# The routers of three expert layers, each as one stage, and one normalisation on GpSimd beside its router

## The reference, cut to what matters

```python
# layer 0: a layer normalisation of the input without gain, and in the layer a second one
mu = mean(x); var = mean((x - mu) ** 2); u = (x - mu) / sqrt(var + 1e-5)
logits = u @ router_W + router_b                    # 1024 x 8
gates = softmax of the two largest logits, at their experts
xhat = (u - mean(u)) / sqrt(var(u) + 1e-5)          # the experts' input
# layer 1
probs = softmax(u @ router_w.T)                     # over all 8
gates = the two largest probs, at their experts
# layer 2
gate = u @ W_gate
mask = softmax(where(gate >= second largest, gate, -inf))
out = mean over the experts of (relu(u @ W1 + b1) @ W2 + b2) * mask
```

## Time and profile before

| | |
|---|---|
| median of 3 runs | 4622.57 us (4617.99 to 4632.91) |
| profiled execution, its own time | 4627.87 us |
| its span, first to last instruction | 4626.1 us |
| mean granted TensorE clock | 0.961 of full speed |
| PE busy | 4177.0 us (90%) |
| PEld busy | 3167.9 us (68%) |
| DVE busy | 2563.9 us (55%) |
| ACT busy | 1782.1 us (39%) |
| POOL busy | 848.0 us (18%) |

### The profile page before, as it was taken

The page is one execution under the profiler, slowest core; times in us unless marked ns, Lnnn a source line. Parts: engine busy times, 40 slices in busy tenths (PEclk is TensorE's granted clock), DMA queues, the critical chain, the costliest instruction groups (busy, mean ns, idle before and its releaser), DMA issues. The chain is left out here.

```text
span 4626.1 us, 107755 instructions
## 1 busy us (share of the span) xinstructions
PE 4177.0 (90%) x44428; PEld 3167.9 (68%) x44428; DVE 2563.9 (55%) x5138; ACT 1782.1 (39%) x3751; POOL 848.0 (18%) x556
## 2 busy tenths in 40 slices
PE   8989999999888989999976789886899999999987
PEld 5669998999667956666642379752699766666465
DVE  4468777777253055555539832246443466665454
ACT  2245555555222424444534312120254344444221
POOL 1222222221101200000029611006222100000201
PEclk9999999999988999999988899898899999999999
DMA  1010000000104821111012168649111000000100
GB/s 35 27 36 18 17 17 17 17 17 1 49 1 174 306 74 44 45 45 45 17 47 78 46 253 314 247 158 141 51 45 54 22 31 24 24 24 10 39 15 10
DMA packets 137827, 305.05 MB, mean 66 GB/s; under 512 B 51800, under 2 KB 87584, under 8 KB 119744
## 3 DMA queue, kind: packets, MB, share of 16 engines
q1 hardware_dynamic: 132992, 287.01, 19.7%
q0 software_dynamic: 4416, 12.06, 0.8%
HBM read 273.46 MB, written 23.47 MB: 64 GB/s over the span
## 5 line engine op out<-in xcount | busy, mean ns | idle before, releaser
L3070 DVE TENSOR_REDUCE block_max<-PS 128x1 f32<-128x512 f32 (+1 forms) x896 | 505.3, 626 | 300.7 <-PE PS L2930 299.9
L3019 ACT ACTIVATE probs_turned<-PS 128x512 f32<-128x512 f32 (+1 forms) x896 | 434.7, 570 | 562.8 <-PE PS L2951 562.7
L1149 PE MATMUL PS<-context_turned,queries 128*128 128x422 f32 (+2 forms) x1536 | 335.3, 360 | 4.8 <-ACT probs L1218 1.9
L1181 PE MATMUL PS<-probs_turned,context_part 128*128 128x256 f32 (+1 forms) x2496 | 327.7, 285 | 2.2 <-DVE weighted L1260 2.2
L1210 ACT CAST probs_turned<-PS 128x512 fp32r<-128x512 f32 (+1 forms) x512 | 232.4, 511 | 229.2 <-PE PS L1161 229.2
L1226 DVE TENSOR_TENSOR probs_turned<-PS,probs_turned 128x512 fp32r<-128x512 f32 (+1 forms) x512 | 276.5, 581 | 75.0 <-ACT probs_turned L1210 73.1
L1181 PEld LDWEIGHTS PS<-probs_turned,context_part 128*128 128x128 f32 (+1 forms) x2496 | 304.2, 189 | 2.4 <-DVE probs_turned L1226 2.4
L2971 PEld LDWEIGHTS PS<-probs_turned,values 128*17 128x17 f32 x13312 | 191.6, 97 | 150.1 <-issue 123.5
L1149 PEld LDWEIGHTS PS<-context_turned,queries 128*128 128x128 f32 x1536 | 262.5, 191 | 32.9 <-ACT probs L1218 9.0
L1218 ACT ACTIVATE probs<-PS,minus_max 128x844 f32<-128x844 f32 (+1 forms) x256 | 238.6, 932 | 105.1 <-DVE minus_max L1271 103.9
L2930 PE MATMUL PS<-keys_turned,queries 32*128 32x512 f32 (+1 forms) x2048 | 241.4, 548 | 40.9 <-ACT probs_turned L3019 35.9
(11 more groups left out here) (542 smaller groups left out, 7507.4 us busy)
## 6 DMA issues: line engine op xcount, KB each, us to landing
context_rows<-in_ctx SPq DMA_DIRECT2D x40, 768.0 KB
context_turned<-ctx_turned SPq DMA_DIRECT2D x32, 800.5 KB
routed_up<-in_L_ffn_W SPq DMA_DIRECT2D x23, 1024.0 KB, 7.9
routed_down<-in_L_ffn_W SPq DMA_DIRECT2D x23, 1024.0 KB, 6.0
routed_up<-in_L_ffn_wg_w SPq DMA_DIRECT2D x23, 1024.0 KB, 7.7
routed_second<-in_L_ffn_w_w SPq DMA_DIRECT2D x23, 1024.0 KB, 10.2
routed_down<-in_L_ffn_w_w SPq DMA_DIRECT2D x23, 1024.0 KB, 5.1
v_all<-v_turned SPq DMA_DIRECT2D x128, 128.0 KB, 17.5
```

What stands on the lines that cost most here:

```text
L1149: last = nc.tensor.matmul(PS[:, j, 0:cols], qs[a][:, v, p * P:(p + 1) * P], yT[b][:, v, at:at + cols], start=(m == 0), stop=(m == 2))
L1181: last = nc.tensor.matmul(O_ps, yp[a][0:kk, u, k, :], probsT[b][0:kk, par, k, :], start=(k == 0 and m == 0), stop=(k == KT - 1 and m == 2))
L3019: nc.scalar.activation(probs[0:kk, t % ring, i, 0:many].rearrange("p k c s -> p (k c s)"), PS[0:kk, bank_of("turned", t, i), 0:many * 2 * ...
L3070: nc.vector.tensor_reduce(part[:, b % 2, chunks[0]:chunks[-1] + 1, i, u // 2], bank, AX_X, ALU.max).then_inc(max_done.sem, 1)
```

## The change

Each router becomes one stage. `Router` issues the sixteen matmuls into one PSUM bank (bank 0, eight columns a tile), signals once, and lets two spare products follow; ScalarE begins the stage with a one-element exponential and later takes the exponential of the scores; VectorE does all the rest, reading the scores from PSUM. `two_of_scores` (layer 0), `two_of_softmax` (layer 1) and `kept_gates` (layer 2) hold VectorE's list. In layer 0 `linear_normal` now keeps moments and both inverse deviations, U takes the plain one, and the stage `normalize(core, U, hat)` is gone: GpSimd makes `hat` from the residual by a subtraction and a multiplication in the router's stage. `uT` of layers 0 and 1 stays allocated for the whole layer. Here is the diff, cut to its core (the lines of `top_two` that went are those described above).

```diff
@@ -447,7 +447,7 @@
                     for t in tiles:
                         if gain is None:
-                            nc.vector.tensor_scalar(dst[:, t, :], X[:, t, :], moments[:, t, 0:1], rstd[:, t:t + 1],
+                            nc.vector.tensor_scalar(dst[:, t, :], X[:, t, :], moments[:, t, 0:1], (both[:, 1] if with_plain else rstd)[:, t:t + 1],
                                                     ALU.subtract, ALU.mult).then_inc(step.sem, 1)
@@ -1727,39 +1727,195 @@
-def top_two(core, own, scores, iota):
...
+class Router:
+    def __init__(self, core, own, w, bias=None):
...
+        self.scores = core.sb(own, "scores", [P, TILES, EXPERTS])
+        self.ready, self.step = core.semaphore("rows_ready"), core.semaphore("vector_step")
+        self.shifted, self.exps = core.semaphore("scores_shifted"), core.semaphore("exps_ready")
+        self.products = core.PS[:, 0, 0:TILES * EXPERTS].rearrange("p (t e) -> p t e", e=EXPERTS)
+    def tensor_program(self, core, pe, src):
+        wait_weights(core, pe)
+        for t in range(TILES):
+            for c in range(DC):
+                last = core.nc.tensor.matmul(core.PS[:, 0, t * EXPERTS:(t + 1) * EXPERTS], src[:, c, t * P:(t + 1) * P], self.w[:, c, :],
+                                             start=(c == 0), stop=(c == DC - 1))
+        last.then_inc(self.ready.sem, 1)
+        spare_products(core, BANKS - 1, 2)
+    def scalar_program(self, core, act, x):
+        core.nc.scalar.activation(self.warm[:], core.ident[0:1, 0:1], ACT.Exp)
+        act.wait_ge(self.shifted.sem, self.shifted.at(1))
+        core.nc.scalar.activation(x, x, ACT.Exp).then_inc(self.exps.sem, 1)
+    def wide(self):
+        return self.top[:].unsqueeze(2).broadcast_to([P, TILES, EXPERTS])
...
+class TopTwo:
...
+    def find(self, core, dve, step, past, scores):
+        nc = core.nc
+        for t in range(TILES):
+            nc.vector.max(self.best[:, t, :], scores[:, t, :]).then_inc(step.sem, 1)
+        dve.wait_ge(step.sem, step.at(past + TILES))
+        for t in range(TILES):
+            nc.vector.max_index(self.place[:, t, :], self.best[:, t, :], scores[:, t, :]).then_inc(step.sem, 1)
+        dve.wait_ge(step.sem, step.at(past + 2 * TILES))
+        nc.vector.tensor_copy(self.placef[:], self.place[:]).then_inc(step.sem, 1)
+    def mark(self, core, dve, step, past):
+        dve.wait_ge(step.sem, step.at(past))
+        for n, out in enumerate((self.first, self.second)):
+            core.nc.vector.tensor_tensor(out[:], self.iota[:].unsqueeze(1).broadcast_to([P, TILES, EXPERTS]),
+                                         self.placef[:, :, n:n + 1].broadcast_to([P, TILES, EXPERTS]),
+                                         ALU.is_equal).then_inc(step.sem, 1)
+def two_of_scores(core, own, src, w, bias, iota, share, X, hat, moments, deviations):
...
     with nc.Block() as block:
         @block.tensor
         def _(pe):
+            router.tensor_program(core, pe, src)
+        @block.gpsimd
+        def _(pool):
+            nc.gpsimd.tensor_tensor(hat[:], X[:], moments[:, :, 0:1].broadcast_to(to), ALU.subtract).then_inc(again.sem, 1)
+            pool.wait_ge(again.sem, again.at(1))
+            nc.gpsimd.tensor_tensor(hat[:], hat[:], deviations[:, 0].unsqueeze(2).broadcast_to(to), ALU.mult).then_inc(again.sem, 1)
+            pool.wait_ge(again.sem, again.at(2))
+        @block.scalar
+        def _(act):
+            router.scalar_program(core, act, share[:])
 
         @block.vector
         def _(dve):
+            wait_weights(core, dve)
+            dve.wait_ge(router.ready.sem, router.ready.at(1))
+            nc.vector.tensor_tensor(scores[:], router.products, bias[:].unsqueeze(1).broadcast_to([P, TILES, EXPERTS]), ALU.add).then_inc(step.sem, 1)
+            dve.wait_ge(step.sem, step.at(1))
+            two.find(core, dve, step, 1, scores)
+            nc.vector.tensor_tensor(share[:], best[:, :, 0:2], best[:, :, 0:1].broadcast_to([P, TILES, 2]),
+                                    ALU.subtract).then_inc(router.shifted.sem, 1)
+            two.mark(core, dve, step, 2 + 2 * TILES)
+            dve.wait_ge(router.exps.sem, router.exps.at(1))
+            nc.vector.tensor_reduce(whole[:], share[:], AX_X, ALU.add).then_inc(step.sem, 1)
+            dve.wait_ge(step.sem, step.at(5 + 2 * TILES))
+            nc.vector.reciprocal(whole[:], whole[:]).then_inc(step.sem, 1)
+            dve.wait_ge(step.sem, step.at(6 + 2 * TILES))
+            nc.vector.tensor_tensor(share[:], share[:], whole[:].unsqueeze(2).broadcast_to([P, TILES, 2]), ALU.mult).then_inc(step.sem, 1)
+    return two.first, two.second
+def two_of_softmax(core, own, src, w, iota):
...
+            nc.vector.tensor_reduce(top[:], router.products, AX_X, ALU.max).then_inc(step.sem, 1)
+            dve.wait_ge(step.sem, step.at(1))
+            nc.vector.tensor_tensor(probs[:], router.products, router.wide(), ALU.subtract).then_inc(router.shifted.sem, 1)
+            dve.wait_ge(router.exps.sem, router.exps.at(1))
+            nc.vector.tensor_reduce(top[:], probs[:], AX_X, ALU.add).then_inc(step.sem, 1)
+            dve.wait_ge(step.sem, step.at(2))
+            nc.vector.reciprocal(top[:], top[:]).then_inc(step.sem, 1)
+            dve.wait_ge(step.sem, step.at(3))
+            nc.vector.tensor_tensor(probs[:], probs[:], router.wide(), ALU.mult).then_inc(step.sem, 1)
+            dve.wait_ge(step.sem, step.at(4))
+            two.find(core, dve, step, 4, probs)
+            two.mark(core, dve, step, 5 + 2 * TILES)
+            dve.wait_ge(step.sem, step.at(7 + 2 * TILES))
...
+def kept_gates(core, own, src, w):
...
+            nc.vector.tensor_reduce(top[:], router.products, AX_X, ALU.max).then_inc(step.sem, 1)
+            nc.vector.tensor_copy(keep[:], router.products).then_inc(step.sem, 1)
+            dve.wait_ge(step.sem, step.at(1))
+            nc.vector.tensor_tensor(gates[:], router.products, router.wide(), ALU.subtract).then_inc(router.shifted.sem, 1)
+            dve.wait_ge(step.sem, step.at(2))
             for t in range(TILES):
+                nc.vector.max(best[:, t, :], keep[:, t, :]).then_inc(step.sem, 1)
+            dve.wait_ge(step.sem, step.at(2 + TILES))
+            nc.vector.tensor_tensor(keep[:], keep[:], spread(best[:, :, 1:2]), ALU.is_ge).then_inc(step.sem, 1)
+            dve.wait_ge(step.sem, step.at(3 + TILES))
+            dve.wait_ge(router.exps.sem, router.exps.at(1))
+            nc.vector.tensor_tensor(gates[:], gates[:], keep[:], ALU.mult).then_inc(step.sem, 1)
+            dve.wait_ge(step.sem, step.at(4 + TILES))
+            nc.vector.tensor_reduce(top[:], gates[:], AX_X, ALU.add).then_inc(step.sem, 1)
+            dve.wait_ge(step.sem, step.at(5 + TILES))
+            nc.vector.reciprocal(top[:], top[:]).then_inc(step.sem, 1)
...
@@ -2492,22 +2648,12 @@
-        logits = core.sb(own, "logits", [P, TILES, EXPERTS])
         share = core.sb(own, "share", [P, TILES, 2])
-        whole = core.sb(own, "gate_sum", [P, TILES])
-        with ExitStack() as front:
-            uT = core.sb(front, "uT", [P, DC, TOKENS])
-            begin(core, tail, X, U, loads=w.loads, turned=(uT, None, None))
-            linear_rows(core, uT, w["L0_ffn_router_W"], logits, w["L0_ffn_router_b"])
-        best, first, second = top_two(core, own, logits, w["iota8"])
-        vector_steps(core, [lambda: v.tensor_tensor(share[:], best[:, :, 0:2], best[:, :, 0:1].broadcast_to([P, TILES, 2]), ALU.subtract)])
-        scalar_step(core, lambda: nc.scalar.activation(share[:], share[:], ACT.Exp))
-        vector_steps(core, [
-            lambda: v.tensor_reduce(whole[:], share[:], AX_X, ALU.add),
-            lambda: v.reciprocal(whole[:], whole[:]),
-            lambda: v.tensor_tensor(share[:], share[:], whole[:].unsqueeze(2).broadcast_to([P, TILES, 2]), ALU.mult)])
-        normalize(core, U, hat)
+        kept = core.sb(own, "moments", [P, TILES, 2]), core.sb(own, "rstd", [P, 2, TILES])
+        uT = core.sb(own, "uT", [P, DC, TOKENS])
+        linear_normal(core, tail, U, loads=w.loads, turned=(uT, None, None), twice=True, kept=kept, with_plain=True)
+        tail.own.close()
+        first, second = two_of_scores(core, own, uT, w["L0_ffn_router_W"], w["L0_ffn_router_b"], w["iota8"], share, X, hat, *kept)
         routed_experts(core, bank, hat, first, second, share, w["L0_ffn_b2"], w["iota8"], ACT.Gelu, skip=U)
 
 
@@ -2518,30 +2664,10 @@
         w = weights(core, own, L1_ffn_router_w=[P, DC, EXPERTS], L1_ffn_w2_b=[EXPERTS, DIM], iota8=[P, EXPERTS])
         bank = RoutedExperts(core, own, "L1_ffn_", "wg_w", "w2_w", "wg_b", "w1_w", "w1_b")
         U = core.sb(own, "u", [P, TILES, DIM])
-        probs = core.sb(own, "probs", [P, TILES, EXPERTS])
-        top = core.sb(own, "top", [P, TILES])
-        with ExitStack() as front:
-            uT = core.sb(front, "uT", [P, DC, TOKENS])
-            begin(core, tail, X, U, loads=w.loads, turned=(uT, None, None))
```

(12 more changed lines are left out.)

103 lines of the change are left out of this document (62 added, 41 removed).

## The result

The changed kernel takes 4607.28 us (median of 7 runs, 4600.83 to 4611.87) against 4627.57 us (7 runs, 4617.99 to 4642.58) of the kernel before on the same chip: ratio 0.9954, interval 0.9936 to 0.9971. It is faster by 20.3 us where 31.6 was forecast, and outside the forecast range. Two parts of that are apart from the mechanism. The forecast stood on a median of three runs, 4622.57; over all 99 runs of the kernel before, these and the ones made with the experiments, the mean is 4627.5 (standard error 0.6). Fourteen runs of the changed kernel have a mean of 4604.9 (1.5). The gain is 22.6 us with a standard error of 1.6, so the miss to explain is 9.0 us, and 4.9 us more of the absolute miss lie in the base.

The account below looks back on a forecast made before the run. It took the sequence of stages, each ending when its slowest engine left, to bound the three router stretches. Savings of 13.7 + 6.4 + 11.5 = 31.6 us from the median 4622.57 gave 4591.0 us; range 4580 to 4604 us.

Parts of the forecast that it names:

- layer 0, normalisation and router: Layer 0: next stage at 1413.4 instead of 1427.72, 14.3 us saved, less 0.6 for the kept deviation: 13.7 us.
- layer 1, router: Layer 1's router, from the last score to the next stage: 4.49 us instead of 10.86, 6.4 us saved.
- layer 2, router: Layer 2's router, from the last score to the next stage: 3.2 us instead of 14.75, 11.5 us saved.
- The unit prices: Router stages: costs per small step, such as 0.27 us for VectorE on 64 PSUM elements and 0.28 for leaving a stage.
- turns of a whole instruction: Layer 0 router: two-SBUF-operand VectorE instructions and GpSimd's take turns by whole instruction, so `share` waits 0.90 us.
- the other case: Layer 0 router: the cast could be held too, putting its 0.23 us behind GpSimd's end, 0.2 us more.
- The clock: Behind the routers: no change taken for TensorE's clock, since the same ten spare products stand before the map product.
- a bound: Layer 0 map product: between 1.8 us less and 1.7 more if TensorE's clock state falls otherwise.
- Rival 2: Expert parts behind the routers: the clock is lower, costing 5 to 13 us, about 4600 us; chance 0.10.
- rival 3: Behind the removed stages: time not returned because something unmoved, such as a transfer, is awaited; two thirds lost, 4612; chance 0.05.
- The range: Whole kernel: 4580 to 4604 us, from the clock's bounds (7 better, 5 worse) and the half spread of the runs.

Follow-up runs that it names:

- the delayed stage: 44 spare products (about 20 us) as a stage ahead of layer 2's mixer: 4616.30 us in the changed kernel, 4639.19 us in the kernel before.
- the covered pauses: Changed kernel with 14 instead of ten spare products before the map (4605.25 us), three more beside `dropT` (4603.51 us), or both (4605.29 us); kernel before with both, 4625.56 us.
- the 18 spare products: Changed kernel with 18 instead of ten spare products ahead of the map product and three more beside `dropT`: 4602.57 us, ratio 0.9943.
- the parts measured alone: Against the kernel before, only layer 0 changed: 4614.29 us, ratio 0.9974; only layers 1 and 2 changed: 4609.72 us, ratio 0.9960.

## Why the prediction was wrong

The direction and the length of the new stages were right; the size was off by 9.0 of 31.6 us. The table compares the start of the same instructions in six profiles of code that is as before in the stretch with nine whose code there is the changed one; the delayed stage, the covered pauses and the 18 spare products are left out where they act. It gives the mean change.

| stretch | forecast | measured |
|---|---|---|
| layer 0, normalisation and router | -13.7 | -11.4 |
| layer 1, router | -6.4 | -6.3 |
| layer 2, router | -11.5 | -11.8 |
| layer 0, map product | 0 | +1.6 |
| layer 1, map product | 0 | -0.6 |
| layer 2, mixer, up to the scan | 0 | +1.6 |
| layer 2, mixer, scan | 0 | +3.8 (standard error 2.1) |
| layer 2, experts | 0 | +1.4 |
| sum | -31.6 | -21.7 |

The table is no full account of the runs' 22.6 us. Where no code differs and no row stands, executions differ as well: from 1485 to 2641 us the six old profiles lie from 3.6 us longer to 6.3 shorter than the first, and those of the changed code from 0.9 to 7.3 shorter.

**The unit prices.** Right. The stages behind the routers took 4.53 and 3.04 us for 4.49 and 3.2. Leaving by VectorE, the one signal, the 64 elements from PSUM in 0.22 to 0.23 us (the forecast took 0.27), the two spare products under VectorE's cover: each as said. The exponential is 0.22 to 0.26 and its signals add 0.1.

**Layer 0.** The new stage is right at full clock, 8.58 us for 8.75. What it replaces was priced too high. The forecast took the 23.07 us from the first router product to the next stage (1404.65 to 1427.72) from one profile. In five of the seven profiles with the old layer 0 the same stretch took 20.15 to 20.35 us, because most of its spare products ran at the full clock: four of them took 1.97 us where the forecast's profile had 3.74. In the forecast's profile and in a repetition:

```profile
1414.62 3.74 PE L134 MATMUL PS<-ident 128*128 128x256 f32 x8 [0.30 <-PEq L698]
```

```profile
1409.37 1.97 PE L134 MATMUL PS<-ident 128*128 128x256 f32 x8 [0.30 <-PEq L698]
```

The granted clock over the stretch behind the products was 0.90 there and 0.75 in the earlier trace rows. The mean of the seven is 21.0 us and that of the twelve with the new stage 9.1, so it gives 12.0 us and not 14.3: 2.0 us of the shortfall lie in the forecast's base. The new stage took 0.7 to 1.0 us longer in seven of the twelve, whose router products ran at the lower clock (5.54 to 5.85 us); with the old layer 0 they never did (3.71 to 3.92). The stretch ahead, `linear_normal`, is not the same code, since it keeps the deviations. With its twelve spare products at full clock (2.75 us) it is 0.45 us longer than before, forecast 0.6. But the list took 3.7 to 4.4 us in ten of the twelve, where in the seven it took 4.0 in three and 2.75 in four, and at 4.44 the last transposes waited some 1.7 us for it.

**GpSimd beside VectorE.** The reading of the earlier trace rows as turns of a whole instruction holds, and the waiting is paid, 1.15 us where 0.90 was taken. But it was laid on `share`, which has two SBUF operands, and fell on the cast, which has one: 1.34 against 0.20 us. The prediction named this as the other case, with 0.2 us more. The Trainium skill, page "SBUF — State Buffer", section "SBUF: two separate sides", says that an operation in a two-port mode takes the shared ports as one with two inputs does. If the cast runs in such a mode, which no run here shows, it is held by that rule, and the trace agrees, 1406.49 to 1407.83 beside GpSimd's end at 1407.78.

**The clock.** This is the step that failed: "I take nothing: before the map stands the same list of ten spare products as before." The list is the same, but it ran faster (6.13 us for 7.19), the pause behind it was longer, and the clock was already at 0.50 when the map product began, where before it fell within it. In twelve profiles with layer 0 changed and fewer than 18 spare products the product took 6.70 to 7.10 us, in six with the old layer 0 and its ten 5.37 to 5.56: nearly the 1.7 us that the forecast had worked out as a bound and not taken. Layer 1 gave 0.6 us back. The same step took the stages that go at the clock of one profile, which is the 2.0 us above. And the bound looked no further than the first products behind the routers. The query products lie some 435 us behind the layer 1 router and took up to 2.5 us more, in either code. Uncovered and unmoved they were dear in all five profiles of the changed kernel and in two of four of the old, and with the cover, or in the one delayed execution, they were not. Rival 2 was this mechanism, at 5 to 13 us with a chance of 0.10. The traces show some 1 us of it in the map products, and 2.3 in layer 0 if the base is counted with it. That is a third of the miss; the rest is not the clock's.

**What does not move.** The second failed step is rival 3's. It let the time go back through a wait for a transfer, and looked for it in the router stretches, where there is none. There are two some 400 us and more behind that of layer 1. The mixer's first product waits for a small load, 1.0 us longer on the mean in the changed code; that is most of the 1.6 us in the table's row up to the scan. Then the scan of layer 2 waits for its loads, and their rate differs from one execution to the next by more than any term of the sum but two: 106.5 to 117.0 us in six profiles of the old code, 111.0 to 117.5 in nine of the changed. The means are 110.9 and 114.7. Three of the six old ones are at 106.5 to 107.7 and none of the nine. It is the largest row of the miss and the least certain; the count over all twenty profiles speaks for a share of the change, and how the change would do it is not shown. The profile that the forecast was built on was one of the fast ones here.

**What stays open.** The 1.4 us in the experts of layer 2. Why the parts measured alone sum to 28.5 to 31.8 us and the whole gives 22.6, and why layer 0 with one other layer misses by 9 and 11 us as well. For the sum of the two parts the difference has a standard error of some 3, and the layers 1 and 2 kernel had a scan of 107.1 us in its profile, 7.6 less than the mean of the changed code, which would be most of it if its other runs were alike. They were not profiled.

**The range.** It held the bounds of the clock but put its centre on a base of three runs that was 4.9 us low; with the base of 99 runs the forecast would have been 4595.9 and the range 4585 to 4609, which holds the result, near its end. Its ends are not made alike either: 4591.0 less 7 and 4 is 4580, but 5 and 4 more is 4600 and not 4604. The half spread of some 7 us was weighed as if it were spread of the measurement. It is a spread of the executions themselves: in the six profiles of the old code the scan differs by 10.5 us, the stretch from 1485 to 2641 us by 9.9, and the first 1388 us by 6.0.

## What to carry to other kernels

Stages of small steps are worth the span between the ends of the engine that does the work, not the busy time, and a sum from rows of the same instructions got the new ones within 0.3 us at full clock. The stages that go need the same care: price them from more than one profile, for here one was 2.0 us above the mean in a single stretch. Behind such a change look at later places where TensorE pauses (1.65 to 4.0 us in the places above): the product behind them came at either level of the clock, so price it at both. Where a long product stands behind a pause, try to fill the pause wholly: 14 spare products that left 2.3 us gained nothing, 18 that left 0.6 us halved the product in the trace, though five runs of the kernel do not tell the gain from noise. Look at each later wait for a transfer as well. And measure the parts in pairs, for parts that are right alone can miss together.

## What the runs showed of the hardware

- TensorE waited for the last of the small loads at the start of one mixer stage for 1.79, 2.40 and 4.04 us in three profiles of the same kernel.
- A VectorE cast of 64 elements from uint32 to float32 in SBUF took 0.19 to 0.20 us alone and 1.34 us beside a GpSimd operation, ending 0.05 us after it; MAX8 and searches beside the same operation took 0.64 us and 0.16 to 0.17, as without.
- A TensorE pause beside a VectorE instruction of 2.26 us cost the sixteen matmuls behind it nothing (7.10 us) in one execution and 2.3 us (9.38) in another of the same program.
- The same 128 loads of 128 KB landed with medians of 17.2 to 20.2 us in executions of the same kernel, at 149 to 151 against 136 GB/s in the middle of the scan.
